# The ordered path of a two-layer graph network on the straight side of its branch, with its loads behind the branch and a shorter pair pipeline in layer 0

## What is computed

```python
h = relu(layernorm(x))                       # [6250, 128]
h = h @ W0.T + b0
x = x + segment_sum(h[src] * edge_weight[:, None], dst, 6250)         # layer 0
h = relu(layernorm(x))
# layer 1: four edge types t, messages, sum per target, GRU gates
m_t = relu(concat(h[src], h[dst]) @ W1[t] + b1[t]) @ W2[t] + b2[t]    # used where edge_type == t
agg = segment_sum(m, dst, 6250)
gi, gh = agg @ W_ih.T + b_ih, h @ W_hh.T + b_hh
r, z = sigmoid(...), sigmoid(...); n = tanh(i_n + r * h_n)
x = x + (1 - z) * n + z * h
```

## Time and profile before

| what | value |
|---|---|
| median of 3 runs | 2180.26 us (2178.88 to 2181.36) |
| device time of the profiled execution | 2183.6 us |
| its span | 2181.9 us |
| mean granted TensorE clock | 0.737 of full speed |
| busy: POOL, PE, DVE, ACT | 1587.4, 1361.2, 877.9, 565.9 us |
| mean DMA rate | 98 GB/s |

### The profile page before, as it was taken

One profiled execution on the slowest core, in us unless ns is written; L12 is line 12 of the kernel. 1 busy time (PEld: TensorE's weight loads), 2 busy tenths in 40 slices (PEclk: granted clock), 3 DMA queues, 4 the chain that ended last, 5 costly groups with the idle time before them and its releaser, 6 DMA issues.

```text
span 2181.9 us, 23718 instructions
## 1 busy us (share of the span) xinstructions
PE 1361.2 (62%) x6752; PEld 1134.7 (52%) x6752; DVE 877.9 (40%) x2467; ACT 565.9 (26%) x1501; POOL 1587.4 (73%) x1678
## 2 busy tenths in 40 slices
PE   2356555555555655655546777767677777776676
PEld 1343444434434434444435667656666666666665
DVE  4732232222322322323134454554545555454554
ACT  2633333332333333333221111111111111111111
POOL 5577777777777777777547777777777777777774
PEclk7556666666666566566667887898888888878888
DMA  7323323323323233233243444444444444444442
GB/s 157 99 55 87 87 79 91 85 77 97 80 78 96 79 85 89 79 91 85 65 116 104 110 110 115 107 114 114 107 115 110 112 111 113 115 106 117 110 111 63
DMA packets 173806, 213.84 MB, mean 98 GB/s; under 512 B 51245, under 2 KB 119564, under 8 KB 173171
## 3 DMA queue, kind: packets, MB, share of 16 engines
q0 software_dynamic: 53248, 109.16, 20.6%
q1 hardware_dynamic: 119179, 102.32, 16.6%
q10 hardware_dynamic: 1244, 0.79, 0.2%
HBM read 176.56 MB, written 35.56 MB: 97 GB/s over the span
## 4 chain that ended last, share of the span: by engine, by line
POOL 67%; issue 22%; DMA 4%; PE 2%; ACT 2%; DVE 1%; SPq 1%; POOLq 0%; DVEq 0%; ACTq 0%
POOL accs L1249 31%; POOL G L1564 15%; POOL edge L1564 15%; POOL g_more L1564 7%; DMA accs<-h_tab,src_t 2%; PE bank L1476 1%; PE bank L1509 1%; DMA base_tab<-base_i 1%; ACT accs L1405 1%; SPq L348 0%; DVE rows L637 0%; ACT accs L1394 0%; ACT accs L1385 0%; ACT hot L1405 0%; DMA p_tab<-hot 0%
## 5 line engine op out<-in xcount | busy, mean ns | idle before, releaser
L1249 POOL DMA_INDIRECT accs<-h_tab,src_t x784 | 741.6, 946 | 252.3 <-issue 235.7
L1476 PE MATMUL bank<-accs 128*125 128x133 f32 x1664 | 352.9, 385 | 328.7 <-ACT accs L1394 250.6
L1476 PEld LDWEIGHTS bank<-accs 128*125 128x125 f32 x1664 | 320.4, 281 | 385.7 <-ACT accs L1394 200.7
L1735 PE MATMUL bank<-qwin,hotT 128*128 128x128 f32 x1664 | 294.6, 331 | 310.2 <-DVE hotT L1629 296.6
L1735 PEld LDWEIGHTS bank<-qwin,hotT 128*128 128x128 f32 x1664 | 249.0, 229 | 351.6 <-DVE hotT L1629 336.7
L1564 POOL DMA_INDIRECT G<-p_tab,src_t x336 | 320.4, 954 | 139.1 <-issue 103.1
L1394 ACT ACTIVATE accs<-accs,edge 128x128 f32<-128x128 f32 x784 | 250.0, 390 | 645.7 <-DMA accs<-h_tab,src_t 645.6
L1564 POOL DMA_INDIRECT edge<-p_tab,src_t x336 | 319.9, 952 | 102.5 <-issue 102.5
L1693 ACT ACTIVATE rows<-rows 128x512 f32<-128x512 f32 x208 | 130.9, 630 | 680.3 <-DVE rows L1637 680.3
L1745 PE MATMUL bank<-hot,rows 128*128 128x128 f32 x1664 | 290.9, 333 | 5.7 <-ACT rows L1693 5.0
L1745 PEld LDWEIGHTS bank<-hot,rows 128*128 128x128 f32 x1664 | 273.5, 249 | 6.1 <-ACT rows L1693 6.0
(11 more groups left out here) (178 smaller groups left out, 1429.1 us busy)
## 6 DMA issues: line engine op xcount, KB each, us to landing
qwin<-q_tab SPq DMA_DIRECT2D x416, 64.0 KB
nodew<-key_tab SPq DMA_DIRECT2D x52, 256.0 KB
nodehot<-key_tab SPq DMA_DIRECT2D x52, 256.0 KB, 3.6
accs<-h_tab,src_t POOLq DMA_INDIRECT x784, 2.6
p_tab<-st SPq DMA_DIRECT2D x25, 250.0 KB
p_tab<-hot SPq DMA_DIRECT2D x25, 250.0 KB
q_tab<-st SPq DMA_DIRECT2D x25, 250.0 KB
q_tab<-hot SPq DMA_DIRECT2D x25, 250.0 KB
```

What stands on the lines that cost most here:

```text
L1249: eng.indirect_dma_start(slot0(o % R0)[:, t, 0:D], None, x if o < EARLY else h0_tab, bass.IndirectOffsetOnAxis(src_t[:, k:k + 1], 0)).then ...
L1476: ins = eng.matmul(pb[SUM_BANK[o % 4]][0:CW, 0:FW], ones_of(o % HR)[:, t, :], slot0(o % R0)[:, t, :], start=t == 0, stop=t == TO - 1)
L1735: ins = eng.matmul(pb[2 + g % 2][:, t * D:(t + 1) * D], hotT[:, g % HT, t * P:(t + 1) * P], qwin[:, g % NG, t // PR, :], start=True, stop= ...
```

## The change

EARLY becomes 7. `choose` tests the opposite value: the number is 1 for the ordered path, the If body is now the ordered path, and the general one is the Else. DVE makes the number with one comparison in place of the same comparison and a later negation. SP's loads of x for the table, the base table's way out and back, the W1/W2 loads and the key store move from the prologue into lists behind the branch; DVE's wait for `basein` moves to step 1 of layer 0. The bias of layer 0 leaves PE and its own small DMA: DVE adds bias times weight sum to the x rows (`bias_rows`). The counts are turned and copied out two steps after the sums, in PSUM and semaphores of their own (`counts_turned`, `counts`). All pair work of PE, ACT and DVE is packed into steps 0, 1 and 2, and on PE and ACT it stands ahead of the step's octet. P, Q go out as 112 and 13 rows each, two DMAs in place of one; the counts store comes last.

```diff
-        EARLY = 6
+        EARLY = 7
...
         def sp_prologue(eng):
...
+            eng.wait_ge(s["qpad"], 1)
+            eng.dma_start(q_tab[N:NPAD, :], zrows[0:NPAD - N, :]).then_inc(s["st_q"], 16)
+            for k in ("st_c", "st_h", "st_p", "upd_st"):
+                eng.sem_inc(s[k], 16)
+
+        def sp_table_rows(eng):
             for i, (a, b) in enumerate(T_PIECES):
                 for h in HALVES:
                     eng.dma_start(t_rows[i][h], x_lin[h, a:b, :]).then_inc(s_t[i], 16)
-            eng.wait_ge(s["b0_set"], 1)
-            eng.dma_start(b0_row[T:T + 1, :], b0.rearrange("(a d) -> a d", a=1)).then_inc(s["b0_in"], 16)
+
+        def sp_bases(eng):
+            eng.wait_ge(s["prep"], 5)
...
+        def sp_weights(eng):
...
+        def sp_base_row(eng):
             eng.wait_ge(s["baseout"], 32)
             eng.dma_start(base_row[:, :], base_tab.rearrange("(a n) -> a n", a=1)).then_inc(s["basein"], 16)
...
+        def sp_keys(eng):
+            eng.wait_ge(s["key16_in"], 1)
+            eng.dma_start(key_tab.rearrange("(p e) -> p e", p=PB), key16).then_inc(s["key_st"], 16)
...
-            seq(eng, eng.tensor_scalar(badp[:, 0:1], pb[4][:, 0:1], 0.5, None, ALU.is_gt))
-            eng.tensor_copy(flag_i[:, :], badp[0:1, 0:1]).then_inc(s["prep"], 1)
-            eng.tensor_scalar(badp[:, 1:2], badp[:, 0:1], -1.0, 1.0, ALU.mult, ALU.add).then_inc(s["prep"], 1)
+            seq(eng, eng.tensor_scalar(badp[:, 1:2], pb[4][:, 0:1], 0.5, None, ALU.is_le))
+            eng.tensor_copy(flag_i[:, :], badp[0:1, 1:2]).then_inc(s["prep"], 2)
...
-        STEPS0 = NOCT + 7
+        STEPS0 = NOCT + 3
...
-        P_SUMS, A_SUMS, P_W0, D_X1, A_ROOT, D_NRM, P_TURN, A_HID, P_P, A_P, P_Q, D_Q = 0, 0, 1, 1, 1, 2, 2, 2, 3, 3, 3, 4
...
+            def bias_rows(p):
+                eng.wait_ge(s["acc0"], 4 * p + 2 * (LAG + 1))
+                eng.wait_ge(s_xl[p % 2], 16 * (p // 2 + 1))
+                for k in range(2):
+                    row = x_in[p % 2][:, k, :]
+                    ins = eng.scalar_tensor_tensor(row, b0bc[0:CW, :], xs[0:CW, 2 * p + k, FW - 1:FW], row, ALU.mult, ALU.add)
+                seq(eng, ins)
...
-                if (p := pair_at(o, D_NRM)) is not None:
-                    normalize(p)
                 if 1 <= o <= NOCT:
+                    if o == 1:
+                        eng.wait_ge(s["basein"], 16)
...
-                if (p := pair_at(o, D_X1)) is not None:
+                if (p := pair_at(o, 0)) is not None:
+                    bias_rows(p)
                     x1_rows(p)
                     variance(p)
-                if (p := pair_at(o, D_Q)) is not None:
+                    normalize(p)
+                if (p := pair_at(o, 2)) is not None:
                     q_out(p)
...
+                eng.activation(sT, pb[4][:, 0:2 * CW], ACT.Copy).then_inc(s["c_sT"], 1)
+
+            def counts(p):
+                eng.wait_ge(s["c_ct"], p + 1)
                 eng.wait_ge(s["st_c"], p * 16 + 16)
-                eng.activation(sT, pb[4][:, 0:2 * CW], ACT.Copy)
-                eng.activation(cnt_pair, pb[4][0:T + 1, 256:256 + 2 * CW], ACT.Copy).then_inc(s["c_sT"], 1)
+                eng.activation(cnt_pair, pb[4][0:T, 256:256 + 2 * CW], ACT.Copy).then_inc(s["c_cnt"], 1)
...
             for o in range(-WEIGHED0, STEPS0):
+                if (p := pair_at(o, 0)) is not None:
+                    sums_out(p)
+                    root(p)
+                if (p := pair_at(o, 1)) is not None:
+                    hidden(p)
+                    p_out(p)
+                if (p := pair_at(o, 2)) is not None:
+                    counts(p)
...
-                    eng.matmul(o, sT[:, k * CW:(k + 1) * CW], w0t[:, :], start=True, stop=False)
-                    ins = eng.matmul(o, cntb[0:T + 1, k, :], b0_row, start=False, stop=True)
+                    ins = eng.matmul(pb[4][0:CW, k * D:(k + 1) * D], sT[:, k * CW:(k + 1) * CW], w0t[:, :], start=True, stop=True)
...
             for o in range(STEPS0):
+                if (p := pair_at(o, 0)) is not None:
+                    sums_turned(p)
+                    times_w0(p)
+                if (p := pair_at(o, 1)) is not None:
+                    turned(p)
+                    rows_of(p, w1a, ("c_qe", p) if p else None, "c_p")
+                if (p := pair_at(o, 2)) is not None:
+                    rows_of(p, w1b, ("c_pe", 2 * p + 2), "c_q")
+                    counts_turned(p)
                 if o < NOCT:
                     octet(o)
...
-                    eng.dma_start(p_tab[c * CW:(c + 1) * CW, :], p_st(k)).then_inc(s["st_p"], 16)
-                eng.dma_start(c_rows[:, 2 * p:2 * p + 2, :], cntb[0:T, :, :]).then_inc(s["st_c"], 16)
+                    for h in HALVES:
+                        eng.dma_start(p_tab[c * CW:(c + 1) * CW, :][h], p_st(k)[h]).then_inc(s["st_p"], 16)
...
-                    eng.dma_start(q_tab[c * CW:(c + 1) * CW, :], q_st(k)).then_inc(s["st_q"], 16)
+                    for h in HALVES:
+                        eng.dma_start(q_tab[c * CW:(c + 1) * CW, :][h], q_st(k)[h]).then_inc(s["st_q"], 16)
+                eng.wait_ge(s["c_cnt"], p + 1)
+                eng.dma_start(c_rows[:, 2 * p:2 * p + 2, :], cntb[0:T, :, :]).then_inc(s["st_c"], 16)
...
-        def choose(eng, general, fast):
+        def choose(eng, fast, general):
...
-            with eng.If(flag):
+            with eng.If(ordered):
+                for f in fast:
+                    f(eng)
...
-            with eng.Else():
-                for f in fast:
                     f(eng)
...
-            choose(eng, [sp_x, sp_store_h0, l0_sp, l1_sp], [f0_sp, f1_sp])
+            choose(eng, [sp_table_rows, sp_bases, sp_weights, sp_base_row, sp_keys, f0_sp, f1_sp],
+                   [sp_weights, sp_keys, sp_x, sp_store_h0, l0_sp, l1_sp])
...
-            eng.wait_ge(s["basein"], 16)
-            choose(eng, [dve_h0, l0_dve, l1_dve], [f0_dve, f1_dve])
+            choose(eng, [f0_dve, f1_dve], [dve_h0, l0_dve, l1_dve])
```

More of the change, by code:

```diff
@@ L343, in sp_prologue @@
                     eng.dma_start(t_rows[i][h], x_lin[h, a:b, :]).then_inc(s_t[i], 16)
-            eng.wait_ge(s["b0_set"], 1)
-            eng.dma_start(b0_row[T:T + 1, :], b0.rearrange("(a d) -> a d", a=1)).then_inc(s["b0_in"], 16)
+        def sp_bases(eng):
+            eng.wait_ge(s["prep"], 5)
+            with nc.allow_non_contiguous_dma(reason="one column of 104 numbers"):
+                eng.dma_start(base_tab[0:NT // PR].rearrange("(p g) -> p g", p=PB), base_i[:, 0:NBLK]).then_inc(s["baseout"], 16)
+                eng.dma_start(base_tab[NT // PR:].rearrange("(p a) -> p a", a=1), base_i[:, NBLK:]).then_inc(s["baseout"], 16)
+        def sp_weights(eng):
             for to, ap in ((w1a, W1[:, 0:D, :].rearrange("t f g -> f t g")), (w1b, W1[:, D:2 * D, :].rearrange("t f g -> f t g")),
@@ L349, in sp_prologue @@
             eng.dma_start(b2s[:, :], b2).then_inc(s["w12_in"], 16)
-            eng.wait_ge(s["prep"], 5)
-            with nc.allow_non_contiguous_dma(reason="one column of 104 numbers"):
-                eng.dma_start(base_tab[0:NT // PR].rearrange("(p g) -> p g", p=PB), base_i[:, 0:NBLK]).then_inc(s["baseout"], 16)
-                eng.dma_start(base_tab[NT // PR:].rearrange("(p a) -> p a", a=1), base_i[:, NBLK:]).then_inc(s["baseout"], 16)
+        def sp_base_row(eng):
             eng.wait_ge(s["baseout"], 32)
             eng.dma_start(base_row[:, :], base_tab.rearrange("(a n) -> a n", a=1)).then_inc(s["basein"], 16)
-            eng.wait_ge(s["qpad"], 1)
-            eng.dma_start(q_tab[N:NPAD, :], zrows[0:NPAD - N, :]).then_inc(s["st_q"], 16)
-            for k in ("st_c", "st_h", "st_p", "upd_st"):
-                eng.sem_inc(s[k], 16)
+        def sp_keys(eng):
+            eng.wait_ge(s["key16_in"], 1)
+            eng.dma_start(key_tab.rearrange("(p e) -> p e", p=PB), key16).then_inc(s["key_st"], 16)
         def sp_x(eng):
-            for k in s_t:
-                eng.wait_ge(k, 32)
             for i, (a, b) in enumerate(PIECES):
@@ L701, in dve_h0 @@
         def dve_h0(eng):
-            before = in_order[0]
             def stats(b):
@@ L720, in dve_h0 @@
             dve_table(eng, range(2, len(TG)))
-            in_order[0] = before
         def pool_h0(eng):
@@ L1449, in f0_act @@
                     table_rows_normal(o + 2)
-                if (p := pair_at(o, A_SUMS)) is not None:
-                    sums_out(p)
-                if (p := pair_at(o, A_HID)) is not None:
-                    hidden(p)
-                if (p := pair_at(o, A_ROOT)) is not None:
-                    root(p)
-                if (p := pair_at(o, A_P)) is not None:
-                    p_out(p)
             eng.wait_ge(s["out0"], NOCT)
@@ L1482, in sums_turned @@
                 if p:
[L1483 removed]
+                    eng.wait_ge(s["c_cnt"], p)
                 for k in range(2):
[L1485 to L1487 removed]
```

(24 more changed lines are left out.)

41 lines of the change are left out of this document (10 added, 31 removed).

## The result

The changed kernel takes 2150.85 us (median, 2150.54 to 2152.2) where the kernel before, timed beside it, takes 2179.57: ratio 0.987 (0.9853 to 0.9887), 28.7 us less. The prediction was 2148.4 in a range of 2143 to 2160. The profiled execution has a span of 2149.4 us.

The account below looks back on a forecast made before the run. POOL's gathers bound the kernel, with three holes around them; -7.1 (start) - 13.3 (table) - 13.0 (gap between layers) + 1.5 (end) = -31.9 us, from the median 2180.26 to 2148.4, range 2143 to 2160.

Parts of the forecast that it names:

- POOL's start: Hole before POOL's first gather, 25.07 us: without jump or queued code fetch, first gather at 18.0, gain 7.1 us.
- The upper bound: On POOL's start: gain 8.4 us if the flag comes 1.34 us earlier, edge weights having the DMA engines to themselves.
- The table: POOL's 13.6 us wait for the table behind its early gathers: DVE starts at 26.5, table lands 76.4, gain 13.3 us.
- The cover of 11.6 us: Layer 0: table landing at 76.4, ahead of the end of POOL's 56 early gathers at 88.0, leaves 11.6 us spare.
- 1.6 to spare: Layer 0: with 48 early gathers POOL would be through at 78.0, still 1.6 us after the table lands.
- The tail: POOL's 36.96 us gap between layers 0 and 1 falls to 23.9, gain 13.0 us (bounds 9.9 and 13.7).
- The end: After the last output SP must jump over the general path, other engines' jumps hidden under its wait: cost 1.5 us.
- (1): Rival, chance 0.12: POOL's start doesn't move, its 8.8 us being something other than the fetch; 2155.5 us.
- (3): Rival, chance 0.06: splitting the P stores between the layers doesn't help, P still lands in 5.75 us; 2151.5 us.
- (5): Rival, chance 0.05: ordered side still jumped to, POOL's fetch stays at 5.58 us, end jump falls away; 2152.5 us.
- (2): Rival, chance 0.08: the table is late, both delays in full leave POOL a wait of 5.4 us; 2153.8 us.
- (4): Rival, chance 0.03: pair work inside the steps stretches four octets beyond 40.0 us; 4 us over gives 2198 us.

Follow-up runs that it names:

- straight kernels: Group of kernels, the changed one and variants, in which POOL reaches the ordered path without a jump; flag to first gather 1.74 to 1.75 us.
- Else kernel: Changed kernel with the ordered path back in the Else body, every engine jumping to it, flag made as before: 2152.71 us, ratio 0.9873.
- 125-row kernel: Changed kernel with P and Q rows stored as 125 rows in one DMA each: 2154.99 us, ratio 0.9885.
- the one with base_row first: Changed kernel with DVE's wait for base_row back at the head of its ordered path: 2156.35 us, ratio 0.9915.
- old-steps kernel: Changed kernel with pair work at its old steps (0 to 4) and behind the octet on PE and ACT: 2155.08 us, ratio 0.9903.
- EARLY = 6: Changed kernel with EARLY set back from 7 to 6: 2149.52 us, ratio 0.9883; on the late chip 2579.75 us, ratio 0.9895.
- the straight side alone: Kernel before with only the ordered path moved to the straight side of the branch, with the flag for it: 2177.85 us, ratio 0.999.
- the four changed kernels: Changed kernel with EARLY = 6, base_row wait first, old pair steps, or SP's Else jump plus P product by halves: 2579.75, 2582.78, 2578.89, 2570.88 us.

## Why the prediction was right, step by step

**POOL's start.** Flag plus 1.75 us, first gather at 17.99 for a predicted 18.0. The size holds: all twelve traces with POOL on the straight side have 1.74 to 1.75. The mechanism, a fetch queued behind the loads, holds for POOL: without them its jump costs 2.2 us, with them 7.1. It doesn't explain DVE's stall, from which the prediction took its price of a jump: that one lay at 42 to 48 us, with the data queue at 16%. The upper bound, a flag 1.34 us earlier, didn't come: the flag's end is 16.24, as before. Taking the x loads out of the prologue didn't bring the edge weights sooner.

**The table.** Predicted DVE start 26.5, seen 25.16; predicted landing 76.4; the last store is issued at 74.83 to 75.57, and the table's 1.9 us more give about 77. The cover of 11.6 us was there (seen 88.5 + 1.2 against 77). Of the threats to it, later loads of the table's rows and a fetch in traffic didn't show. Gathers that share the engines with the loads did: DVE waited 5.0 us for the first octet, and the table's way is 2.0 us longer than the 49.9 it was taken for. That the landing came out within 1 us is luck, since DVE also started 1.3 us early. The sum is right but EARLY = 7 had no part in it, as the working's "1.6 to spare" with 48 gathers already said.

**The tail.** Gap 24.18 for a predicted 23.9: landing 2.75 for 2.6, and the steps to the last P store as worked out. The bound for 125 rows was too low: 6.46 and not 5.75. The split is worth 3.7 us of landing and, with one more issue ahead of it, 2.9 of the gap.

**The end.** +1.5 predicted, +3.1 seen, of two causes that the prediction didn't part. The first is the jump. From the end of DVE's last operation to the end of the span it takes 2.4 us before and 3.6 after (3.2 to 3.6 in the straight kernels of these chips, 2.4 in the Else kernel): +1.2, near the 1.5. The way there was not the predicted one, so the nearness is luck. SP's own jump is 0.3 of it. Another 0.2 or so is PE's jump, which starts with its last matmul, lasts 3.9 us and ends after SP's; the prediction had the other engines' jumps hidden under SP's wait. The largest part, 0.6, is that SP waits 2.3 us for the last output store to land where it waited 1.7. The instruction packets of the jumps move in the same stretch, but no run shows that they delay the store.

The second cause is the clock. From the start of the last gather to the end of DVE's last operation it takes 18.2 us before and 20.3 after. In that stretch PE works on the last two chunks, and the granted clock was different. The last 10 to 3 us of the spans, columns as in the earlier trace rows, of the kernel before, of the changed one and of the 125-row kernel:

```profile
2171.90:2178.90 7.00, 3.92 (x24) 3.11 (x22) 2.86 (x10) 1.70 (x5) 0.00 (x0) 1.00 0.08 21
```

```profile
2139.40:2146.40 7.00, 3.46 (x14) 2.98 (x14) 2.10 (x7) 1.02 (x3) 0.00 (x0) 0.74 0.04 10
```

```profile
2143.30:2150.30 7.00, 3.00 (x19) 2.08 (x17) 2.53 (x9) 1.30 (x4) 0.00 (x0) 1.00 0.05 15
```

A clock of 1.00 is the upper level, 2.4 GHz. Of the ten traces of these chips the three with 1.00 (the two here and the one with base_row first) have 17.9 to 18.2 us from the last gather to DVE's last operation, the three with 0.74 to 0.76 have 19.8 to 20.3, and the four at the lower level, 0.50, have 20.6 to 20.7. The same two products of the last chunk take 0.22 us in the kernel before and 0.43 in the changed one. PE did the same work ahead of it in all of them, the groups of layer 1 and then the last two chunks, and the clock stood now at one level and now at the other, with straight kernels on all sides. So the 2.0 us are not the change's, as far as ten traces can tell. The prediction has no term for the clock.

**POOL's first gathers.** Two of them are long in the changed kernel, 1.52 and 1.98 us in place of 0.95:

```profile
19.43 1.52 POOL L1248 DMA_INDIRECT accs<-in_x_dram,src_t  x1 [0.30 <-issue]
...
23.77 1.98 POOL L1248 DMA_INDIRECT accs<-in_x_dram,src_t  x1 [0.30 <-issue]
```

They cost 1.6 us, and the prediction has no term for them: it took the gathers at their steady distance. They are the second and the fifth in every straight kernel, with the loads ahead of the branch as well as behind it, so the place of the x loads isn't the cause. The Else kernel, whose POOL starts 2.3 us later, has one (1.77); the kernel before, whose POOL starts 7 us later, has none. What it is in those 6 us is open.

**From 32.5 to 28.7.** The gathers of the profiled execution of the kernel before take 947 ns, those of the changed one 944 (medians, and the line above), with distances of 1.2508 and 1.2490 us. Over the layers this is the -2.5 us of layer 1 and 1.5 of layer 0. It isn't the change's: layer 1, in which every kernel gathers alike, takes 1042.9 to 1046.2 us in the ten traces; the old-steps kernel has 947, the EARLY = 6 one 944. Without these 4 us the trace says 28.5, and the medians say 28.7. That they agree so well is luck in part: 2.0 us at the end, the other way, aren't the change's either, and without them too the trace says 30.5. At which clock the other runs ended isn't known. So of the 3.2 us by which the sum missed, the long gathers are 1.6; the rest lies within what differs from run to run, and the end's own term was, if anything, too large (1.2 for 1.5).

**The rivals.** (1) POOL's start doesn't move, (3) the split doesn't help and (5) no straight layout are out by the traces. (2) needs 11.6 us of delay, and moving the wait alone, which makes DVE 18.9 us later, shows how it would look: 5.1 us of wait. (4), pair work inside the steps as a brake, didn't happen: POOL waits on the octet sums once, 0.3 us.

## What to carry to other kernels

When one engine's steady stream bounds a kernel, add up its holes, and ask of each what comes last there after the edit: the straight side alone gave 2.4 us in the medians, all of it through DVE, and POOL's start with the table 20 in the traces. A jump at a runtime branch cost each engine something else here, 0.4 us on SP, 2.2 on POOL and 5.5 on DVE, and more with the data queue full, so put the path that runs on the straight side; where an engine must jump, keep big loads behind it. Look at the end too, where the other side must be jumped over and the slowest engine's jump counts. And see which share of the DMA engines a store gets: 125 rows took 29% of them, 112 and 13 rows 82%.

## What was not expected of the hardware

On one of the chips, the late one, all kernels took 20% longer (before 2607.63 us). POOL's own time per gather was the same, 944 to 947 ns, but in the EARLY = 6 kernel it waited 142 us in layer 0 for something that the trace calls remote and 242 us in layer 1 for DVE's sums, which wait for gathered rows. The DMA rate over the span was 83 GB/s against 99. POOL is not the bound on that chip, and still the four changed kernels gained 25 to 37 us of 2607 there, perhaps because the holes that the change closes are there on any chip; no trace of the kernel before was taken there. What delays the gathers was not looked into either.
